# Attention with 32-row tiles of one head, its warm-up ahead of the first score, and its weighing behind four scores

## The reference

```python
q = _rope(proj(Wq, bq)); k = _rope(proj(Wk, bk)); v = proj(Wv, bv)
scores = jnp.einsum('bhtd,bhsd->bhts', q, k) / scale
attn = jax.nn.softmax(scores, axis=-1)
out = jnp.einsum('bhts,bhsd->bhtd', attn, v)
```

## Time and profile before

| What | us |
| --- | --- |
| three runs | 2863.02, 2863.93, 2864.11 |
| median | 2863.93 |
| the profiled execution | 2837.83 |
| its span, first to last instruction | 2836.5 |
| PE busy in the span | 2165.7 (76%) |
| DVE busy | 2123.1 (75%) |
| ACT busy | 1456.9 (51%) |
| POOL busy | 504.2 (18%) |

### The profile page before, as it was taken

The page is one execution under the profiler, slowest core; times in us unless marked ns, Lnnn a source line. Parts: engine busy times, 40 slices in busy tenths (PEclk is TensorE's granted clock), DMA queues, the critical chain, the costliest instruction groups (busy, mean ns, idle before and its releaser), DMA issues. The chain is left out here.

```text
span 2836.5 us, 39102 instructions
## 1 busy us (share of the span) xinstructions
PE 2165.7 (76%) x13128; PEld 1149.2 (41%) x13128; DVE 2123.1 (75%) x4605; ACT 1456.9 (51%) x2898; POOL 504.2 (18%) x410
## 2 busy tenths in 40 slices
PE   6888955853279999999998559999999999449920
PEld 5667744741133333333332323333333333249910
DVE  6667657644569999999994668999999998375635
ACT  4443430421017777777777106777777777304510
POOL 2223300756600000000000330000000000005644
PEclk9989965986659999999999768999999999758965
DMA  4000000342320000000000330000000000202211
GB/s 171 0 0 0 0 29 8 91 89 84 101 80 25 15 23 24 13 25 13 25 1 1 104 124 13 24 13 25 24 13 24 13 13 2 89 15 60 68 46 52
DMA packets 64544, 109.19 MB, mean 38 GB/s; under 512 B 10352, under 2 KB 44272, under 8 KB 64112
## 3 DMA queue, kind: packets, MB, share of 16 engines
q1 hardware_dynamic: 55408, 88.60, 9.2%
q0 software_dynamic: 8960, 18.37, 2.9%
HBM read 64.46 MB, written 41.94 MB: 38 GB/s over the span
## 5 line engine op out<-in xcount | busy, mean ns | idle before, releaser
L1039 DVE TENSOR_REDUCE mh<-psum 128x1 f32<-128x512 f32 x2048 | 1276.0, 684 | 135.8 <-PE psum L922 121.1
L1019 ACT ACTIVATE p<-psum 128x512 f32<-128x512 f32 x2048 | 1072.9, 603 | 331.3 <-PE psum L956 331.3
L956 PE MATMUL psum<-qs,ks 64*128 64x512 f32 x2048 | 750.0, 449 | 88.7 <-ACT p L1019 88.7
L922 PE MATMUL psum<-ks,qs 64*128 64x512 f32 x2048 | 775.1, 464 | 35.0 <-DMA ks<-qk_parts 34.3
L956 PEld LDWEIGHTS psum<-qs,ks 64*128 64x128 f32 x2048 | 331.4, 185 | 714.9 <-ACT p L1019 695.5
L966 PE MATMUL psum<-p,v_ext 128*32 128x512 f32 x4096 | 548.0, 607 | 31.7 <-ACT p L1019 31.7
L922 PEld LDWEIGHTS psum<-ks,qs 64*128 64x128 f32 x2048 | 342.0, 190 | 79.3 <-DMA ks<-qk_parts 34.7
L157 PE MATMUL psum<-ident,xn 128*128 128x128 f32 x160 | 44.4, 455 | 262.1 <-DVE xn L125 218.2
L575 ACT ACTIVATE hid<-psum,stage 128x128 f32<-128x128 f32 x448 | 132.5, 367 | 181.2 <-PE psum L545 181.2
L519 POOL DMA_INDIRECT x_in<-n_rows,token_of x152 | 167.4, 1102 | 250.7 <-POOLq L78 183.7
L966 PEld LDWEIGHTS psum<-p,v_ext 128*32 128x32 f32 x4096 | 81.0, 108 | 188.4 <-ACT p L1019 184.1
(11 more groups left out here) (172 smaller groups left out, 2405.8 us busy)
## 6 DMA issues: line engine op xcount, KB each, us to landing
qs<-qk_parts SPq DMA_DIRECT2D x128, 100.0 KB
ks<-qk_parts SPq DMA_DIRECT2D x128, 100.0 KB
answers<-y_out SPq DMA_DIRECT2D x152, 64.0 KB, 1.5
qk_parts<-qh SPq DMA_DIRECT2D x16, 512.0 KB, 4.4
qk_parts<-kh SPq DMA_DIRECT2D x16, 512.0 KB, 4.3
ew<-in_moe SPq DMA_DIRECT2D x1, 5136.0 KB, 18.1
ew<-in_moe SPq DMA_DIRECT2D x1, 4624.0 KB, 13.9
n_rows<-xn SPq DMA_DIRECT2D x8, 512.0 KB, 3.2
```

What stands on the lines that cost most here:

```text
L922: pe.matmul(psum[:, bank, :], a["qs"][r, g % NKF, i * P:(i + 1) * P], a["ks"][r, g % NKF, j % KM, k * HALF:(k + 1) * HALF], start=True, st ...
L956: pe.matmul(psum[:, S_BANK + n % NS, :], a["ks"][r, g % NKF, j % KM, i * P:(i + 1) * P], a["qs"][r, g % NKF, h * HALF:(h + 1) * HALF], sta ...
L1019: act.activation(a["p"][:, n % NP, :], psum[:, S_BANK + n % NS, :], ACT.Exp, scale=DH ** -0.5)\
L1039: dve.tensor_reduce(a["mh"][:, g % 2, c, k:k + 1], psum[:, bank, :], AX.X, ALU.max).then_inc(used, 1)
```

## The change

Three edits. KT goes from 64 to 32, so that KM is 1: each head has a tile of 32 rows of its own, `ks` has one plane, and no rows of another head are multiplied with zeros. The eight matmuls of 256 columns among the last lead maxima go; six of 512 columns stand between the last lead maximum and the first score. The weighing of step s-1 moves from behind score 1 and its maximum to behind score 3 and its maximum, ahead of what else the plan has for the step.

```diff
-KT = 64
+KT = 32
 KM = KT // GR
...
-WARM = 8
+WARM = 6
...
-            for n, f in enumerate(first):
+            for f in first:
                 fill(f)
-                if n >= len(first) - 2 * WARM and n % 2:
-                    pe.matmul(psum[:, S_BANK, 0:HALF // 2], w.att[layer][5], t["y_t"][:, 0:HALF // 2], start=True, stop=True)
+            for n in range(WARM):
+                pe.matmul(psum[:, S_BANK, :], w.att[layer][5], t["y_t"][:, 0:HALF], start=True, stop=True)
             for s in range(nsteps):
                 todo = list(plan[s])
                 score(s, 0)
                 more(todo)
                 score(s, 1)
                 more(todo)
-                if s:
-                    weigh(s - 1)
                 score(s, 2)
                 more(todo)
                 score(s, 3)
                 more(todo)
+                if s:
+                    weigh(s - 1)
                 for f in todo:
                     fill(f)
             weigh(nsteps - 1)
```

## The result

The changed kernel takes 3115.88 us, median of four runs (3031.56 to 3230.32), against 2864.02. The ratio is 1.065, with an interval of 1.058 to 1.072; the forecast was 3012 us, 1.052. Its time varies from run to run as its granted clock does, with means of 0.74 to 0.82 against 0.872, and the ratio is taken over the runs that this disturbed least. The profiled execution took 3175.69 us (span 3174.4, clock 0.76), 337.9 more than that of before.

What follows compares the result with a forecast made beforehand. The prediction took a chain through TensorE and ScalarE, 2.67 us a step, to bound the kernel. Terms -41 + 25 + 1 = -15, plus 154 for lost clock and 9, gave +148: 3012 us, range 2840 to 3300.

Steps and rivals of the forecast that it cites:

- (b, c): Per layer: 28 copy steps, half falling, 22 us; two that miss the output transposes and wait eight steps, 21 us.
- The chain: Plain step at full clock, from first score to the next step's, through TensorE and ScalarE: 2.59 us against 2.67.
- The -41: Saving from the shorter plain step, -0.08 us each over 512 steps: -41 us, bounds -92 and 0.
- The extras: Once in eight steps, transposes of maxima and outputs and ScalarE's copy: 1.21 for 0.80, 62 times, +25 us.
- The warm-up: Ahead of each layer's first score: first score at about 838 against 837.57, +1 us for both layers.
- The clock: Granted clock partly lost in the attention steps: 77 us per layer, 154 for two; chance of partly slow clock 0.64.
- (a): Start of each layer: clock falls before the first weighing, low until second output transposes, 17 steps; 15 x 1.29 = 19 us.
- (d): Tail of each layer, with half of the former score rows, at half clock: 12 x 1.29 = 15 us.
- half clock nearly throughout: Rival: output transposes don't lift the clock; 85% of 512 steps slow, +561, 3425 us; chance 0.15.
- Full clock throughout: Rival: six warm-up matmuls start the stage at 2.4 GHz and the weighing keeps it: 2846 us, faster; chance 0.17.
- Four tiles at once: Rival: score and maximum pairs behind the weighing pack closer on four tiles; step 2.49, 2798 us; chance 0.04.

Runs made afterwards that it cites:

- both at 64 rows: The changed kernel with KT put back to 64, so moved weighing and new warm-up together: 2909.21 us, ratio 1.014.
- full-array pad of 128 columns: The changed kernel plus one useless full-array matmul of 128 columns in each step that has maxima: 2989.64 us, ratio 1.039.
- 32-row pad: The changed kernel plus one useless 128-column matmul on a 32-row tile in each step that has maxima: 3036.57 us, ratio 1.055.

## Why the prediction was right, and where its steps were off

The verdict, slower through a clock lost in part, and the range held; 3012 lies some 1.3% under the ratio's 3050 (1.065 x 2864), 3.3% under the median. That it lies so near is partly luck, as (b, c) below show: too many falls, each too short.

**The chain, forecast 2.59, is 2.67.** Two terms were too small: score to weighing 0.44 for 0.41 (the upper bound was 0.49), and score to exponential 0.60, where I took 0.54 from the third score of a step. Before the first exponential of a step ScalarE waits for two things, the weighing three steps back and the score; whether that makes the 0.06 was not tried. The -41 is 0.

**The extras** are +0.21 for the transpose of maxima, as forecast; 0.51 for the copy (0.58 forecast); 0.59 for the transposes of outputs (0.42). In the run of both at 64 rows they make +34 us for two layers (2 x 17.2), where +25 was forecast: nearly right.

**The warm-up**: first maximum to first score 35.9 us (822.76 to 858.64) and 36.7 us in the two layers, for 35.1: +2 for both, where +1 was forecast.

**The clock.** At half clock a plain step is 4.13 (3.96 forecast), 1.46 over the full-clock step.
(a) Start: the clock fell where I said, between warm-up and first weighing, but came back after 5 and 9 steps, not 17. Of the 38 us for two layers, 18 came (the excess over 2.67 a step, less that of before).
(b, c) Copy steps: the place was right, the way wrong. I had 28 falls, 24 of which end with the next output transposes; there were 8, six in the first layer and two in the second, and most stayed down for a group or more: 109, 14, 143, 14, 79 and 143 us in the first layer, 61 and 143 in the second. The middle steps cost 268 us more than before in this execution, extras included, where the terms came to 2 x 43 + 25 = 111. In shorter runs it must have been less, as 3031.56 leaves 168 for all. So the failed term is the time spent at half clock behind a fall, which I tied to the next output transposes by one case in the earlier trace rows. It held once there; with half the rows none of the eight falls ended with the transposes right behind it.
(d) Tail: 29 us for 30.

The rivals: half clock nearly throughout is excluded by the 319 steps at full clock. Full clock throughout is what the 64-row tiles give with the same order and warm-up, at 2909, so even it was not on the faster side. Four tiles at once gave nothing visible: 2.67 with 32 rows and with 64.

By the edits: the tiles alone cost 7.1%, the order 1.4%, the warm-up nothing, and all three together 6.5%. They don't add, since the tiles' loss in the old order is a late start, and in the new order falls at copy steps. The moved weighing thus matters twice at 32 rows: it is there that copy steps fall, as none did in the traces of the old order. What shortens the start, from 69 steps to 5 and 9, is open: at 32 rows the new warm-up and the new order were run only together.

TensorE was busy 3.38 of the 4.20 us before the fall at 913, and it was idle for at most 0.54 us at a stretch ahead of any of the eight falls. Around the copy steps at 64 rows the longest idle time is 0.54 us too, and there the clock held. The Trainium skill ("TensorE: Matmul & The Clock Gate", section "Why this matters for your kernels") names idle gaps between bursts as what lets the clock fall. The traces here show falls without long gaps; 64-row tiles with the same gaps, or 32-row tiles with a full-array matmul in them, went without a fall before the tail. What decides that one copy step falls and the next, alike, doesn't, stays open; so does why executions differ.

## What to carry to other kernels

A smaller matmul tile that skips multiplications with zeros can be slower: look at the granted clock of the whole run, and of several runs, before counting the saved rows. When a long entry sits in an in-order queue between two users of a small ring of banks, moving it only moves the chain; cutting it in two pieces, with the ring's users between them, takes half of it off the chain (-2.6% here). Price a chain through an in-order engine with that engine's own pace between the hand-overs.

## What the runs showed of the hardware that was not expected

The same steps ran for long at either clock: 32-row tiles in the old order at half clock for 69 steps and at full for 176, in both layers. The full-array pad of 128 columns kept the clock where the 32-row pad of equally many did not. In one order, with a copy step of 3.18 us in which TensorE was busy 2.53 and 2.52 us, the clock fell eight times with 32-row tiles and in no copy step with 64-row ones. A weighing of 256 columns took 0.64 us and one of 512 columns 1.07, with eight instructions each.
